# Layer-norm statistics: the bf16 copy on ScalarE instead of VectorE, and first weight loads behind gates

## What is computed

```python
xn = layernorm(x)                                  # x: 4 x 4096 x 1024, f32
q, k, v = split(xn @ Wqkv + bqkv)                  # 1024 each
kv  = sum over t of (k / |k|) * v                  # one row of 1024 per batch
att = ((q / |q|) * kv) @ Wout + bout
h   = silu(xn @ w1.T * w1_s) * (xn @ w2.T * w2_s)  # 4096 wide
h   = gelu(h @ h1.T * h1_s)
h   = gelu(h @ h2.T * h2_s)
out = x + att + h @ w3.T * w3_s
```

## Time and profile before

| | us |
|---|---|
| Median of 2 runs | 3002.85 |
| Their range | 2993.78 to 3011.91 |
| The profiled execution, device time | 2994.01 |
| Its span on core 0, the slowest | 2992.5 |
| Busy: TensorE | 2836.9 (95%) |
| Busy: ScalarE | 452.9 (15%) |
| Busy: VectorE | 369.4 (12%) |

### The profile page before, as it was taken

How to read it: one execution, slowest core, us unless ns; L and a number is a source line. 1 busy time by engine, 2 the same in 40 slices (tenths; PEclk the granted TensorE clock), 3 DMA queues, 4 the chain that set the end, 5 groups by cost and what they waited for, 6 DMA issues and landing times.

```text
span 2992.5 us, 30165 instructions; the slowest of 8 cores (2961.4 to 2992.5 us)
## 1 busy us (share of the span) xinstructions
PE 2836.9 (95%) x12764; PEld 1274.7 (43%) x13024; DVE 369.4 (12%) x429; ACT 452.9 (15%) x452; POOL 219.9 (7%) x420
## 2 busy tenths in 40 slices
PE   2996999999999999999997999999999999999998
PEld 0332444444444444444443444444444444444443
DVE  3363211550000000000002121100000000000011
ACT  1553211531000000000000131110000000000000
POOL 0000000110000000000000000000000000000000
PEclk8997999999999999999998999999999999999999
DMA  4544344984444444444446643444444444444454
GB/s 107 119 97 95 57 81 73 159 130 83 74 76 77 78 78 76 74 77 77 78 82 130 139 72 71 80 76 78 77 74 75 77 78 78 77 75 75 77 113 105
DMA packets 71412, 260.04 MB, mean 87 GB/s; under 512 B 8176, under 2 KB 8304, under 8 KB 71280
## 3 DMA queue, kind: packets, MB, share of 16 engines
q0 software_dynamic: 59904, 218.13, 44.3%
q1 hardware_dynamic: 11376, 39.97, 4.6%
HBM read 466.74 MB, written 9.44 MB: 159 GB/s over the span
## 4 chain that ended last, share of the span: by engine, by line
PE 85%; DMA 4%; DVE 1%; issue 1%; ACT 1%; SPq 0%; DVEq 0%; ACTq 0%
PE PD L198 24%; PE PC L198 23%; PE PB L198 19%; PE PA L198 19%; DMA xs<-x_fm 2%; DMA out_fm<-os 1%; DVE os L753 1%; DMA wr<-wqkv_t 0%; DVE os L747 0%; ACT os L719 0%; DVE Gb L211 0%; SPq L757 0%; ACT Gb L582 0%; DVE Ab L532 0%; ACT L609 0%
## 5 line engine op out<-in xcount | busy, mean ns | idle before, releaser
L198 PE MATMUL PC<-Gb,wr 128*128 128x512 bf16 x2038 | 473.1, 382 | 25.1 <-DVE Gb L275 22.5
L198 PE MATMUL PD<-Gb,wr 128*128 128x512 bf16 x2041 | 470.3, 380 | 2.3 <-issue 0.2
L198 PE MATMUL PB<-Gb,wr 128*128 128x512 bf16 x1690 | 389.6, 381 | 5.9 <-DVE rstd_b L254 4.1
L198 PE MATMUL PD<-Ab,wr 128*128 128x512 bf16 x1503 | 351.8, 385 | 26.7 <-ACT os L719 24.9
L198 PE MATMUL PA<-Gb,wr 128*128 128x512 bf16 x1508 | 345.4, 379 | 1.6
L198 PE MATMUL PC<-Ab,wr 128*128 128x512 bf16 x1505 | 345.3, 379 | 1.7
L198 PEld LDWEIGHTS PC<-Gb,wr 128*128 128x128 bf16 x2080 | 202.9, 98 | 274.7 <-issue 32.0
L198 PEld LDWEIGHTS PD<-Gb,wr 128*128 128x128 bf16 x2080 | 203.8, 98 | 247.2 <-issue 3.2
L198 PEld LDWEIGHTS PB<-Gb,wr 128*128 128x128 bf16 x1728 | 169.3, 98 | 210.4 <-issue 7.7
L191 POOL DMA_DIRECT2D wr<-h_t x256 | 135.1, 528 | 1616.6 <-PE PB L198 766.5
L198 PEld LDWEIGHTS PD<-Ab,wr 128*128 128x128 bf16 x1536 | 151.5, 99 | 213.5 <-issue 38.0
(11 more groups left out here) (88 smaller groups left out, 984.3 us busy)
## 6 DMA issues: line engine op xcount, KB each, us to landing
wr<-h_t POOLq DMA_DIRECT2D x256, 512.0 KB, 5.1
wr<-w_t POOLq DMA_DIRECT2D x96, 512.0 KB, 5.7
xs<-x_fm SPq DMA_DIRECT2D x56, 512.0 KB, 6.3
wr<-wqkv_t POOLq DMA_DIRECT2D x56, 512.0 KB, 7.2
out_fm<-os SPq DMA_DIRECT2D x16, 512.0 KB, 3.1
wr<-wout_t POOLq DMA_DIRECT2D x8, 512.0 KB, 6.6
ustats_scratch<-u_b SPq DMA_DIRECT2D x1, 512.0 KB, 8.7
ustats_scratch<-rstd_b SPq DMA_DIRECT2D x1, 512.0 KB, 8.4
```

What stands on the lines that cost most here:

```text
L198: e.matmul(p[:, h * 512:(h + 1) * 512], l, r, start=a, stop=b),
```

## The change

The copy of line 211 becomes an activation with the function Identity on ScalarE, with ScalarE's semaphore as its token. It keeps its waits (the load of x, and the last matmuls that read this region of `Gb`). This holds for all four calls of `plan_stats`. `dma_w` gets one more optional wait, `gate`. The four K weight units of tile 0 are now issued right after the statistics of tile 0 are planned, the first with no gate, the others behind the column-sum matmuls of chunks 1, 3 and 5; the four V units of tile 0 are issued behind those of chunk 7, and `plan_proj` takes them ready. The order of units in the ring of five buffers stays the same.

```diff
--- before.py
+++ after.py
@@ -186,10 +186,10 @@
                        waits=[ftok], inc=xs_ring.semn[j])
             return j, slot, tok
 
-        def dma_w(unit_ap):
+        def dma_w(unit_ap, gate=None):
             j, slot, ftok = w_ring.next()
             tok = S.op("gpsimd", lambda e, o=slot, i=unit_ap: e.dma_start(out=o[:, :], in_=i),
-                       waits=[ftok], inc=w_ring.semn[j])
+                       waits=[ftok, gate], inc=w_ring.semn[j])
             return j, slot, tok
 
         def mm(ps_name, hs, lhsT, rhs, start, stop, waits=(), inc=None):
@@ -208,9 +208,9 @@
                     pend.pop(0)()
                 jx, xslot, tx = dma_x(c, t0)
                 if via_region:
-                    tb = S.op("vector", lambda e, g_=g, c_=c, i=xslot: e.tensor_copy(
-                        xn_sl(g_, c_), i[:, :]),
-                        waits=[tx, war[REGION[g]]], inc="s_dv")
+                    tb = S.op("scalar", lambda e, g_=g, c_=c, i=xslot: e.activation(
+                        xn_sl(g_, c_), i[:, :], AF.Identity),
+                        waits=[tx, war[REGION[g]]], inc="s_ac")
                     sq_src = xn_sl(g, c)
                 else:
                     jb, bslot, fb = xb_ring.next()
@@ -230,6 +230,7 @@
                                inc="s_pe" if hh == 1 else None)
                 if via_region:
                     chunk_toks[c] = [tok_s, tq]
+                    st["chunk_toks_%d" % g] = chunk_toks
                 else:
                     xb_ring.set_free(jb, [tok_s, tq])
 
@@ -402,6 +403,9 @@
                     st["kv_dve_par0"] = st["kv_done"]
 
             plan_stats(0, "PA", "PB")
+            ck0 = st["chunk_toks_0"]
+            st["pre_k"] = [dma_w(wqkv[4, :, :])] + [
+                dma_w(wqkv[4 + i, :, :], gate=ck0[2 * i - 1][0]) for i in (1, 2, 3)]
             xn_toks_g[4] = xn_toks_g[0]
             for t in range(NT1):
                 kbuf = qkvt if t % 2 == 0 else kB2
@@ -455,6 +459,10 @@
 
                 plan_proj([(wqkv[4 + i, :, :], [2 * i, 2 * i + 1]) for i in range(4)],
                           t, k_evac, pre=st.get("pre_k"))
+                if t == 0:
+                    st["pre_v"] = [dma_w(wqkv[8 + i, :, :],
+                                         gate=st["chunk_toks_0"][7][0])
+                                   for i in range(4)]
                 while pend_n:
                     pend_n.pop(0)()
                 if t == 0:
@@ -467,7 +475,7 @@
                 if t == NT1 - 1:
                     plan_qproj(4)
                 plan_proj([(wqkv[8 + i, :, :], [2 * i, 2 * i + 1]) for i in range(4)],
-                          t, v_evac)
+                          t, v_evac, pre=st.pop("pre_v", None))
                 war[t % 3] = S.pe_tok()
                 st["pre_k"] = ([dma_w(wqkv[4 + i, :, :], ) for i in range(4)]
                                if t + 1 < NT1 else None)
```

## The result

| | before | changed |
|---|---|---|
| Median of all runs, us | 3003.68 (21) | 3022.66 (22) |
| Lowest, us | 2988.18 | 3008.16 |
| Ratio to before | 1 | **1.005, 95% interval 1.0028 to 1.0072** |

In some executions of either kernel the cores of a die run at a lower clock and take some per cent longer; the ratio leaves these out, and by it the change costs 15 us (8 to 22), against the 18 of the prediction's sum. The interval lies above 1, so the loss is real, and it is far under 2%.

A forecast was written before the change was run, and what follows sets the result against it. TensorE waits for layer-norm statistics in four plan_stats calls; -5.3+12.0+1.5+8.0+0.7+1.3 = +18.2 us gave 3012 from the profiled execution or 3021 from the median, so 3016 was taken, range 2998 to 3036.

The forecast's parts named there:

- start: First plan_stats call: held-back weights let x load sooner, gain 5.7, less 0.4 for the longer copy: -5.3 us.
- second call: After K of tile 0: copies wait behind Exp on ScalarE, six loads become exposed, V later by +12.0 us.
- clock behind it: V after the second call begins at the lower clock, 1.2 GHz: +1.5 us, between 0 and 3.
- third call: After K of tile 1: copies behind ScalarE's Exp, paced by buffer turns, Q later by +8.0 us.
- fourth call, with the clock behind the third: Start of second part: later buffer release and longer copy, +1.3 us; lower clock after the third call, +0.7.
- 36.0 for the last copy: First call: chunk 7's copy expected at 36.0 us, between 35.5 and 37.7, a gain of 5.7.
- my estimate for the start: First call, if DMA engines take turns between queue rows: a gain of about 4 us rather than 5.3.
- A landing of 4.1: Second and third calls: x load time assumed between 3.5 and 4.9 us, giving a buffer turn of 5.5.
- A (loads slow): Second and third calls: x landings of 6.3, turn 7.7, +18.5 and +14.5; 3027 to 3036 us; chance 0.13.
- B (not slower): Start gains 15 us, later calls fall to ScalarE bounds +8.7 and +5.2; 2994 to 3000 us; chance 0.08.
- D (weights late): Gates hold K's weight units past their need: +8 us, 3024 us; chance 0.05.
- C (V wholly at 1.2 GHz): Low clock stays through all of V after the second call: +27.6 us, near 3042; chance 0.04.

The follow-up runs named there:

- after_3x: The changed kernel with a third x buffer in place of two unused buffers; ratio to before 1.0035 (1.0018 to 1.0052).
- gates_only: The changed kernel with every copy back on VectorE, so only the gates on the weight loads remain; ratio to before 0.9967 (0.9954 to 0.998).
- best: Changed kernel with copies on VectorE, third x buffer, first weights behind chunk 7, fourth call's three x chunks loaded before the barrier, its weights behind chunk 7; ratio 0.9877.
- gates_3x: gates_only with a third x buffer; no ratio measured, first FFN matmul at 284.5 us (before 300.0).

## Why the prediction was right

**Direction and size.** Forecast within 2% and slower, 3016 us, with a sum of +18.2; measured +15 (8 to 22) by the ratio, +18.9 at the first FFN matmul in the median of the cores, +16.5 on core 0. By its steps, median of the cores:

| step | predicted | measured |
|---|---|---|
| start | -5.3 | -4.8 (statistics begin at 39.7, before 44.5) |
| second call | +12.0 | +11.9 |
| clock behind it | +1.5 | +1.1 (V's first matmul to the next Exp 64.2, before 63.1) |
| third call | +8.0 | +8.6 |
| fourth call, with the clock behind the third | +2.0 | +0.3 |

Of the 1.8 us left to 18.9, 0.8 lie between the start of the statistics and the first Exp (64.7, before 63.9); the rest comes from adding medians of different cores.

**Start.** The total came out, in part by luck: two terms were both too small, and their errors cancelled. My 36.0 for the last copy had 1.6 us of ScalarE's queue in it (chunk 1 at 14.4 instead of 12.8), so the gates alone were given 7.3 (5.7 and 1.6). Alone, they brought the last copy from 41.6 to 33.0, a gain of 8.6, and the copy's place took not 1.6 but 2.9 of it back. I had charged ScalarE's queue only for chunks 0 and 1; the last copy stands also behind the square of chunk 6 (1.1 us).

By the rule of the Trainium skill, "DMA: Bandwidth & Descriptors", section "Queues, rings and completion order", that a DMA engine takes turns between queue rows, my estimate for the start was a gain of about 4; my sum had 5.3. The measured 4.8 lies between, and no run here separates them.

**Second and third call.** The mechanism held in the order given: the copies wait behind Exp, two chunks are there, and the other six pass through two buffers. A landing of 4.1 was assumed and 3.7 to 4.6 measured, a turn of 5.5 against 5.6. after_3x confirmed what ScalarE alone would take, 19.0 to 19.8 behind Exp, with 19.7. There is a slip in the recorded sum for V: its terms (128.5, 2.3 and 0.6) make 131.4, or +11.5, and not 131.9. On core 0 copy 7 began at 124.94 and V at 128.65, 3.7 later, where these terms have 2.9; with that the +12.0 comes out.

**Clock.** On core 0 V's first group took 4.78 us, +1.2 over 3.62; in the median of the cores 4.6 against 3.6. Behind the third call I had added 0.7. Core 0 alone would deny that term: Q's first group took 4.02 there, before 4.42. But the median of the cores is 5.0, before 4.4, so some 0.5 of it is there, inside the distance from Q to the FFN. What this distance grew by in all is 0.3, so the +1.3 for the fourth call doesn't show in it; at this size the scatter hides both. On core 0 the clock was back at 2.4 GHz within the first group of V and of Q, as before, although the whole wait now ran at the lower level.

**Rivals.** A (loads slow) fell: no x load of the two exposed calls took over 4.6 us on core 0, or over 4.8 on any core. B (not slower) needed landings below 3.2; the fastest were 3.6 in the third call of core 0 and 3.4 on any core. D (weights late) fell: TensorE's waits at K are those for VectorE's normalized chunks, 22.5 us in both kernels. C (V wholly at 1.2 GHz) happened on no core: six were at 2.4 GHz behind V's first group, and the two others follow in the last section.

## What to carry to other kernels

An engine's long waits say little about whether its work should move. VectorE waited 99.6 us for loads here, and the 19.3 of the second call cost nothing, because they passed during a projection. Moving the casts behind ScalarE's evictions put them into the time in which TensorE waits. In the second call this cost 9.6 us because ScalarE then did both the copy and the square of each chunk there, and 2.3 because the loads, whose buffers the copies free, started only then. So ask of an operation that is to move what stands ahead of it in the new queue, and what waits for the buffer that it frees.

Where a stage is bound by DMA work, order the loads by when they are needed. In gates_only four weight units were held back; the first of them is used by a matmul only 81 us into the program before (core 0), and the FFN began 10 us sooner. In the fourth call, loading three chunks of x ahead of the barrier and the weights behind chunk 7 brought 12.8 us (Q to FFN 86.6 in best, 99.4 in gates_3x).

## What was not expected of the hardware

On cores 2 and 3 of the changed kernel's profile the granted clock of long busy stretches was that of neither level (0.5 or 1.0 of full) but a mean of 0.8. Core 2 by stretches (the wait between them is left out), and its matmuls in K of tile 0:

```profile
72.00:113.00 41.00, 35.58 (x130) 14.22 (x130) 1.24 (x2) 19.44 (x18) 2.11 (x4) 0.84 0.31 52
...
135.60:211.00 75.40, 71.83 (x273) 29.38 (x271) 44.24 (x51) 31.20 (x29) 4.22 (x8) 0.81 0.42 84
```

```profile
84.05 4.38 PE L198 MATMUL PC<-Gb,wr 128*128 128x512 bf16 x16
88.78 4.38 PE L198 MATMUL PD<-Gb,wr 128*128 128x512 bf16 x16
```

Sixteen matmuls take 4.38 us instead of 3.62, one group like the next, and V's first matmul to the end of the next Exp takes 75.8 us instead of 63.1. From 345 us on the clock is 1.00. This is why core 2 ended last: its FFN begins at 338.3, and from there it takes 2689.5 us, much as core 0. The low clock began in K of tile 0, ahead of the waits that the change lengthened, so they did not bring it about.

Nor does it take a copy on ScalarE. In gates_only cores 6 and 7 show the same from 110 to 180 us, a granted clock of 0.81 and groups of sixteen matmuls in 4.38 us, while cores 4 and 5 have 0.98 and 0.97 there. Both times it was a pair of neighbouring cores. The cause stays open, and no run was made for it.
